# Maxima ahead of the FFN products in batch 1's slots of a fused attention and FFN kernel

## What is computed

```
xn = layernorm(x)
q, k, v = (proj(Wq), proj(Wk), proj(Wv))
scores = einsum('bhqd,bhkd->bhqk', q, k) / sqrt(32)
scores = where(causal, -inf, scores)
ctx = softmax(scores) @ v
s = ctx @ Wo.T
hidden = fwht(silu(xn @ W1.T) * (xn @ W3.T))
g = silu(hidden @ W2.T)
out = x + s * g
```

## Time and profile before

| | us |
|---|---|
| median of 3 runs | 928.82 (928.81 to 930.75) |
| the profiled execution | 929.33 |
| its span | 927.6 |
| TensorE busy in the span | 917.1 (99%) |
| VectorE busy | 710.5 (77%) |
| ScalarE busy | 611.6 (66%) |
| GpSimd busy | 291.7 (31%) |

### The profile page before, as it was taken

The page is one execution under the profiler, slowest core; times in us unless marked ns, Lnnn a source line. Parts: engine busy times, 40 slices in busy tenths (PEclk is TensorE's granted clock), DMA queues, the critical chain, the costliest instruction groups (busy, mean ns, idle before and its releaser), DMA issues.

```text
span 927.6 us, 18915 instructions
## 1 busy us (share of the span) xinstructions
PE 917.1 (99%) x6541; PEld 528.1 (57%) x6541; DVE 710.5 (77%) x1413; ACT 611.6 (66%) x1281; POOL 291.7 (31%) x528
## 2 busy tenths in 40 slices
PE   8999999999999999999999999999999999999998
PEld 7864655665655656854444445555555555585445
DVE  7787999899899898766664569898989989843344
ACT  4558889998888877852443337788777887833231
POOL 1896664556556344000000002322323223310000
PEclk9999999999999999999999999999999999999999
DMA  9797356656346413672115411121211212150111
GB/s 292 277 254 257 104 156 171 177 143 163 107 120 168 125 48 99 232 256 84 46 57 176 134 38 42 47 75 42 82 41 58 64 41 65 46 205 23 46 46 46
DMA packets 64974, 107.91 MB, mean 116 GB/s; under 512 B 6640, under 2 KB 27760, under 8 KB 64368
## 3 DMA queue, kind: packets, MB, share of 16 engines
q1 hardware_dynamic: 64880, 106.72, 37.7%
HBM read 72.94 MB, written 33.55 MB: 115 GB/s over the span
## 4 chain that ended last, share of the span: by engine, by line
PE 71%; ACT 3%; DVE 2%; issue 1%; DMA 1%; POOL 0%; ACTq 0%; POOLq 0%; DVEq 0%
PE f L1801 25%; PE f L1586 7%; PE f L1585 7%; PE f L1587 7%; PE s L1758 5%; PE m L1738 3%; PE o L1776 3%; PE m L1881 3%; PE xs L1738 1%; PE o L1778 1%; PE m L1886 1%; DMA qk_st<-m_lo 1%; DVE p_lo L1417 1%; ACT stages L976 1%; PE s L1853 1%
## 5 line engine op out<-in xcount | busy, mean ns | idle before, releaser
L1417 DVE TENSOR_TENSOR p_lo<-stages,p_hi 128x512 f16<-128x512 f32 (+2 forms) x288 | 193.8, 681 | 22.1 <-ACT p_hi L986 21.2
L1801 PE MATMUL f<-x_hi,w_lo 128*128 128x512 f16 x512 | 194.6, 380 | 0.0
L1801 PE MATMUL f<-x_lo,w_hi 128*128 128x512 f16 x512 | 194.4, 380 | 0.0
L1801 PE MATMUL f<-x_hi,w_hi 128*128 128x512 f16 x512 | 193.9, 379 | 0.0
L986 ACT ACTIVATE p_hi<-stages 128x512 f16<-128x512 f32 (+2 forms) x288 | 160.2, 556 | 24.9 <-ACT stages L976 13.6
L777 POOL TENSOR_SCALAR_AFFINE_SELECT stages<-stages 128x128 f32<-128x128 f32 x192 | 68.3, 361 | 264.6 <-ACT stages L976 264.1
L1758 PE MATMUL s<-qk_st 98*128 98x512 f32 (+6 forms) x384 | 118.6, 383 | 1.2 <-ACT stages L976 0.3
L976 ACT ACTIVATE stages<-s,qk_back 128x512 f32<-128x512 f32 x144 | 88.2, 613 | 30.3 <-PE s L1758 29.5
L1400 DVE CUSTOM_DVE_ANT_0 m<-m,causal 128x1024 f32<-128x1024 f32 (+1 forms) x98 | 104.4, 1066 | 1.2 <-PE m L1738 1.2
L1100 ACT ACTIVATE h_hi<-hidden 128x1024 f16<-128x1024 f32 x32 | 33.9, 1058 | 95.8 <-PE f L1587 95.8
L1487 DVE TENSOR_TENSOR h_lo<-hidden,h_hi 128x1024 f16<-128x1024 f32 x32 | 39.2, 1224 | 75.1 <-ACT h_hi L1100 75.1
(11 more groups left out here) (291 smaller groups left out, 1876.4 us busy)
## 6 DMA issues: line engine op xcount, KB each, us to landing
qk_st<-qk_parts SPq DMA_DIRECT2D x48, 256.0 KB, 4.6
w<-w1w SPq DMA_DIRECT2D x16, 512.0 KB, 4.3
scan<-w1w SPq DMA_DIRECT2D x12, 512.0 KB, 5.0
qk_st<-qk_parts SPq DMA_DIRECT2D x48, 128.0 KB, 2.6
wht_in<-w SPq DMA_DIRECT2D x4, 1024.0 KB, 10.9
qk_parts<-qk_hi SPq DMA_DIRECT2D x16, 256.0 KB, 3.2
qk_parts<-qk_lo SPq DMA_DIRECT2D x16, 256.0 KB, 4.9
w_butterflied<-wht_in SPq DMA_DIRECT2D x4, 1024.0 KB, 6.1
```

Of the source, the lines that this page charges most:

```text
L1417: dve.tensor_tensor(p_lo[s][:], expd[q % NE][:, 0:end - need], p_hi[s][:], ALU.subtract).then_inc(p_lo_done, 1)
L1801: mm = pe.matmul(F[m][:, 0, :], w, v, start=k == 0, stop=k == GMM - 1)
```

## The change

Only in batch 1, a slot's maxima are issued ahead of its FFN products instead of behind them. Scores stay first, contexts stay behind the FFN products, and batch 0 keeps its order.

```diff
                     at = ffn_upto(g - 1)
                     kept = 1 if (g in CTX_PLAN or b == 0 and g in MAX_PLAN) and g < SLOTS else 0
-                    some_ffn(at, ffn_upto(g) - kept)
+                    if b == 0:
+                        some_ffn(at, ffn_upto(g) - kept)
                     for jm, r in MAX_PLAN.get(g, []):
                         maxima(n0 + jm, r)
+                    if b > 0:
+                        some_ffn(at, ffn_upto(g) - kept)
                     for first, end in CTX_PLAN.get(g, []):
```

## The result

| | before | after |
|---|---|---|
| median (5 runs each, measured together) | 930.75 us (928.81 to 930.83) | 938.31 us (937.04 to 939.51) |
| the profiled execution | 929.33 | 937.04 |
| its span | 927.6 | 935.3 |

The ratio is 1.0079, with a 95% interval of 1.0064 to 1.0094: slower by 7.6 us on the medians (6.0 to 8.7 by the interval). Forecast were 8.8 us more and 937.6 us.

The account below looks back on a forecast made before the run. TensorE, busy 258.43 of 259.00 us in batch 1's heads, was taken to bound the kernel. 14 heads at 0.61 us (8.5) plus 0.3 for the first gave 8.8 us more, 937.6 us, range 934.5 to 941.5.

Parts of the forecast that it names:

- Part 2: Batch 1, slot 10: maximum r=1 on TensorE waits for VectorE's m_lo, 0.58 us (0.53 to 0.63).
- release price: Time from the end of VectorE's work to the start of the waiting TensorE matmul: 0.05 to 0.15 us, taken as 0.10.
- The anchor on scores 6: m_lo ends 5.86 us after TensorE's own scores 6, unchanged, so the wait returns in every head.
- Part 3: Slot 11: maximum r=2 needs the reduction of r=0, 0.61 us later; behind r=1's wait it adds only 0.03 us.
- Part 4: Slot 1: maximum r=4 needs the reduction of r=2, 0.55 us, less than TensorE's lateness of 0.61; adds nothing.
- none ahead of r=3 to r=7: Sign: after the first head, TensorE shows no wait for VectorE's reductions ahead of maxima r=3 to r=7.
- Part 5: FFN groups that ended ahead of a maximum end at most 0.43 us later; costed at nothing, covered by ScalarE's queue.
- Part 6: Heads 2 to 15: 14 times 0.61 us, 8.5 us; the first head adds 0.3 us (0.15 to 0.4).
- Not slower: Rival: earlier products let VectorE, and m_lo with it, run ahead; 928.3 us at best; chance 6%.
- The adding up of waits: Rival: waits of r=1, r=2 and r=4 add to 1.74 us a head, 953.5 us; 6% together with a partial form.
- The clock: Rival: pauses of 0.6 us every 17 us drop TensorE to 1.2 GHz of 2.4; 954 us; chance 4%.
- A shorter wait: Rival: p_lo of step 7, ahead of m_lo, comes down by 0.2 us; about 0.4 a head, 934.7 us; chance 8%.

Follow-up runs that it names:

- r=1 alone: Kernel before, with only maximum r=1 issued ahead of its slot's FFN products in batch 1: period 17.00 us, median 937.5 us, ratio 1.0078.
- two products passed: Kernel before, with each maximum of batch 1 passing two FFN products of its slot instead of all: period 16.61 us, median 931.0 us, ratio 1.0008.
- r=4 alone: Kernel before, with only maximum r=4 issued ahead of its slot's FFN products in batch 1: period 17.02 us, median 936.81 us, ratio 1.0067.
- the last kernel: Kernel before, all maxima but r=4 ahead in batch 1; VectorE makes m_lo and the reduction of r=0 ahead of p_lo: 930.73 us, ratio 1.0010.
- all but r=1 ahead: Kernel before, with every maximum except r=1 issued ahead of its slot's FFN products in batch 1: period 17.07 us, median 937.94 us, ratio 1.0072.

## Why the prediction was right, step by step

- **What bounds.** Right. TensorE has no slack in batch 1, and the whole wait reached the end: the 14 periods took 7.9 us more, with the first head 8.4, of which 7.7 show in the span.
- **Part 2, r=1.** The mechanism was right: a wait for m_lo, 14 times, in the place named. The release price was 0.05 us in the heads (669.02 to 669.07), the lower bound and not the middle of 0.10 that I took. With it the wait is 0.53, as r=1 alone shows (17.00 - 16.47).
- **The anchor on scores 6.** Right: 5.85 us against 5.86, and the wait came back in every head.
- **Part 3, r=2.** Right in kind, since it adds only some 0.03 to r=1. A head lost 0.56 to 0.57 us in place of 0.61, again by the release price.
- **Part 4, r=4.** Right, and shown by running it alone: 0.51 us in the 10 heads where nothing hides it, nothing in the change. The margin was as thin as computed (0.61 against 0.55): in every head of the change the weight load of r=4 did wait, 0.26 us, though its matmul did not. That goes against the sign "none ahead of r=3 to r=7" read strictly. The least that the four others had in hand was 0.87 us (r=6: 657.75 against 656.88), not 0.9; nothing hangs on it.
- **Part 5, later FFN groups at nothing.** Right: the five other maxima ahead cost nothing in time or period, apart from about 0.6 us in the first head.
- **Part 6, the first head.** 0.3 us was forecast; from its first scores to scores 6 it took 560.98 - 552.88 = 8.10 us against 7.64 before, 0.46 more. The wait of r=6, for which I allowed up to 0.2, was the larger share.
- **Sum.** 8.8 us forecast; 7.6 us between medians, 8.4 within batch 1's heads. The middle value of the release price is the term that was too large: 14 x 0.05 = 0.7 us less with the lower bound, and 0.15 more for the first head. That 937.6 us came within 0.7 us of the measured 938.31 is in part luck: I added to a median of 928.82, and the five runs of the kernel before, which stand near 928.8 or near 930.8 us, have 930.75. The 1.9 us more there and the 1.2 us less in the difference nearly cancel.
- **The rivals.** "Not slower" fell: m_lo came no sooner after scores 6 (5.85 us). The adding up of waits is excluded, by the three kernels with one maximum each. The clock stayed at 1.00. A shorter wait did not occur in the change, but its mechanism, shorter p_lo, appeared where VectorE's order was changed; I had written that nothing moves what runs beside them, which holds for the change and not for that experiment.
- **The rule on the spacing.** The trace does not agree with the 131 ns of the Trainium skill, TensorE: Matmul & The Clock Gate, section Back-to-back issue gap. By it, as an estimate, two products passed would have cost nothing (0.26 us moved, 0.30 or more in hand). They cost 0.14 us a head, as the row's 0.216 says.

## What to carry to other kernels

On an engine that is full, moving an instruction ahead gains nothing unless somebody waits for its result; first read what it needs, and its slack in the kernel before is how far it may move, as long as the other engines keep their order (here one product free, the second already paid for). Waits in one loop that hang on the same anchor (here scores 6 of each head) overlap: the loop paid the largest, so three faults cost as much as one, and removing the one that the profile names only handed it to the next.

## What the hardware showed unexpectedly

VectorE's p_lo and GpSimd's sums and products, which each read two operands from SBUF, hardly ran side by side: the one that started first took its normal time and the other grew, p_lo from 0.69 to 0.89 us and L796 on GpSimd from 0.40 to 0.89. The Trainium skill, SBUF — State Buffer, section SBUF: two separate sides, describes this as an exclusive lock on a shared pair of ports: the one that starts first holds it for the whole instruction, and the other blocks. The trace agrees on who waits. What is held back shows here as a longer instruction, and a little less than the whole overlap was lost: p_lo grew by 0.2 us where the two overlap by 0.34 us, L796 by 0.49 where they overlap by 0.62.

In some kernels the scores of a head's first step waited for the stored m_lo, in a few heads and not in all. With r=4 alone the weight loads waited 5 times for it, up to 1.0 us, where the kernel before had no such wait in batch 1:

```profile
PEld s L1758 <- DMA qk_st<-m_lo: 3.6, 5, 1.0
```

It stands in the four slower heads there (17.04 to 17.28 us, the others 16.97 to 16.99), in the two of 16.96 us in the last kernel and in the one of 17.43 us with all but r=1 ahead. In the kernel before these scores start 2.74 us after m_lo ends, in the changed one 3.31 us; in the four heads of r=4 alone they started after 3.30 to 3.54 us. So in those four heads the transfer needed more than the 2.74 us that the kernel before leaves it; a wait of TensorE between m_lo and the scores leaves it more. What delays the transfer in those heads was not tried and stays open.
